# The last cross-attention of a two-layer decoder: exponentials and values split into leads and rests, products with the values in three single passes

## The reference

```python
x = _layernorm(x, ln_media_w, ln_media_b)          # the 77 context rows
lat = _layernorm(latents, ln_lat_w, ln_lat_b)      # the 512 decoder positions
q = lat @ Wq + bq
kv_in = jnp.concatenate([x, lat], axis=1)          # 589 keys and values
kv = kv_in @ Wkv + bkv
k, v = jnp.split(kv, 2, axis=-1)
...
sim = jnp.einsum('bhid,bhjd->bhij', q * scale, k)  # 16 heads of width 64
sim = sim - jax.lax.stop_gradient(jnp.max(sim, axis=-1, keepdims=True))
attn = jax.nn.softmax(sim, axis=-1)
out = jnp.einsum('bhij,bhjd->bhid', attn, v)
...
return out @ Wout + bout
```

## Time and profile before

| | |
|---|---|
| three runs | 1129.16, 1139.89, 1142.47 us; median 1139.89 |
| the profiled execution | 1145.58 us, span 1143.9 us |
| first step to last step of the pipeline | about 418 to 1056 us of the span |
| PE busy over the span | 1060.7 us, 93% |
| DVE, ACT, POOL busy | 724.1, 577.2 and 248.6 us |
| chain of work that ended last, share by engine | PE 85%, DVE 10%, ACT 3%, POOL 1% |

### The profile page before, as it was taken

How to read it: one execution, slowest core, us unless ns; L and a number is a source line. 1 busy time by engine, 2 the same in 40 slices (tenths; PEclk the granted TensorE clock), 3 DMA queues, 4 the chain that set the end, 5 groups by cost and what they waited for, 6 DMA issues and landing times.

```text
span 1143.9 us, 14143 instructions
## 1 busy us (share of the span) xinstructions
PE 1060.7 (93%) x4746; PEld 734.1 (64%) x4746; DVE 724.1 (63%) x1640; ACT 577.2 (50%) x1057; POOL 248.6 (22%) x307
## 2 busy tenths in 40 slices
PE   6869999999999479999989999999999999999896
PEld 3648779888888256565657666676666676665532
DVE  5866575656656567768675776756767657752256
ACT  4336444342334345565554665646665646655453
POOL 6111220008447241212131111111111111110001
PEclk9978667999999679999999999999999999999998
DMA  7100000000001000000000000000000000000001
GB/s 230 7 1 1 1 1 1 1 1 1 1 1 37 1 1 1 1 1 0 1 1 1 1 1 1 1 1 1 1 1 1 1 1 1 1 1 1 1 0 38
DMA packets 15667, 9.87 MB, mean 9 GB/s; under 512 B 8760, under 2 KB 14828, under 8 KB 15084
## 3 DMA queue, kind: packets, MB, share of 16 engines
q1 hardware_dynamic: 15595, 8.96, 2.7%
HBM read 7.60 MB, written 1.05 MB: 8 GB/s over the span
## 4 chain that ended last, share of the span: by engine, by line
PE 85%; DVE 10%; ACT 3%; issue 1%; POOL 1%; POOLq 0%; DVEq 0%; ACTq 0%
PE PS L1459 81%; PE PS L1471 4%; DVE mxm L1349 1%; DVE st L988 1%; DVE X_ODD L999 1%; DVE X_EVEN L999 1%; DVE BIG L1082 1%; DVE mx L1079 1%; DVE QA L1292 1%; POOL rs L564 0%; DVE mv L991 0%; ACT BIG L725 0%; ACT BIG L717 0%; PE PS L1821 0%; DVE VXA L1308 0%
## 5 line engine op out<-in xcount | busy, mean ns | idle before, releaser
L1459 PE MATMUL PS<-BIG,VXA 128*128 128x512 f32 (+1 forms) x640 | 335.6, 606 | 0.0
L943 ACT ACTIVATE BIG<-PS 128x512 f32<-128x512 f32 (+1 forms) x320 | 189.7, 593 | 136.0 <-PE PS L1459 126.0
L1349 DVE TENSOR_REDUCE mxm<-PS 128x1 f32<-128x512 f32 x256 | 170.6, 687 | 95.7 <-PE PS L1459 91.1
L1459 PE MATMUL PS<-QA,KA 128*128 128x512 f32 (+1 forms) x320 | 194.8, 609 | 0.0
L1459 PEld LDWEIGHTS PS<-BIG,VXA 128*128 128x128 f32 (+1 forms) x640 | 115.2, 190 | 29.4 <-ACT BIG L943 8.5
L1459 PE MATMUL PS<-QB,KB 128*128 128x512 f32 (+1 forms) x320 | 126.2, 394 | 0.0
L1459 PE MATMUL PS<-KA,QA 128*128 128x512 f32 (+1 forms) x512 | 118.0, 333 | 8.0 <-DVE mxm L1349 7.0
L905 ACT ACTIVATE KA<-PS,b1s 64x78 fp32r<-64x78 f32 (+1 forms) x128 | 64.3, 502 | 90.9 <-PE PS L1459 89.2
L1459 PEld LDWEIGHTS PS<-KA,QA 128*128 128x128 f32 x512 | 86.5, 190 | 31.8 <-DVE mxm L1349 11.7
L666 POOL CAST KA<-KA 64x78 fp32r<-64x78 f32 (+1 forms) x128 | 55.0, 429 | 205.2 <-ACT KA L905 201.4
L666 POOL CAST QB<-QA 64x512 fp32r<-64x512 f32 x64 | 39.0, 609 | 268.8 <-ACT QA L905 268.6
(11 more groups left out here) (251 smaller groups left out, 1791.5 us busy)
## 6 DMA issues: line engine op xcount, KB each, us to landing
X_EVEN<-in_x SPq DMA_DIRECT2D x4, 256.0 KB, 3.3
VXA<-in_L_ffn_Wg SPq DMA_DIRECT2D x1, 1024.0 KB, 5.7
VXA<-in_L_ffn_Wu SPq DMA_DIRECT2D x1, 1024.0 KB, 7.7
VXA<-in_L_ffn_Wd SPq DMA_DIRECT2D x1, 1024.0 KB, 9.3
REG<-in_L_xattn_Wkv SPq DMA_DIRECT2D x1, 1024.0 KB, 4.7
QB<-crow SPq DMA_DIRECT2D x64, 2.0 KB
out<-X_EVEN SPq DMA_DIRECT2D x4, 256.0 KB, 2.3
wq1s<-in_L_xattn_Wq SPq DMA_DIRECT2D x1, 512.0 KB, 8.5
```

The lines of the kernel that those rows point to most:

```text
L943: act.activation(PX[0:rows, g % 4, :], PS[0:rows, g % 2, :], ACT.Exp, scale=SCALE_W).then_inc(pw_ready, 1)
L1349: dve.tensor_reduce(mxm[:, p % 2, h, m:m + 1], PS[:, 2 + g % 2, :], AX.X, ALU.max).then_inc(mu_free, 1)
L1459: return pe.matmul(dst, lhsT, rhs, start=start, stop=stop, **kw)
```

## The change

- **Exponentials.** Each slot's exponential is still written as float32 (`PX`), and now also as a lead `PHI` of type `fp32r`. In six of the ten slots ACT makes it by a second `Exp` of the same scores (`lead_act`); in slots 2, 3, 7 and 8 (`LEAD_ON_VECTOR`) DVE makes it by a copy of `PX`. POOL subtracts the two into the rest `PLO` (`rest`), once per slot, behind that slot's `twins`.
- **Products with the values.** `pv` is three single-pass matmuls (value rest times `PHI`, value lead times `PHI`, value lead times `PLO`), and it comes three slots behind the scores (`LAG`). The third waits for POOL's `rest`. `s_wide` waits for ACT's second exponential of two slots before, where ACT makes one.
- **Values.** They are made a quarter of the heads at a time (256 columns), 20 tasks per sequence where there were 10 of 512 columns. ACT writes their lead (`value_lead`), DVE the rest (`value`).
- **Places.** `c` moves from slot 6 to 7, `yE` from 6 to 8, the inverse sums (`HEAD_SLOTS`) from slots 2 and 7 to 3 and 8, and the maximum units are spread so that two of them come before their step.

```diff
-HEAD_SLOTS = {2: 1, 7: 0}
-MAX_UNITS = {0: [0], 1: [1, 2], 2: [3, 4], 3: [5, 6], 4: [7], 5: [8, 9]}
+LAG = 3
+HEAD_SLOTS = {3: 1, 8: 0}
+MAX_UNITS = {0: [2], 1: [3], 2: [4], 3: [5], 4: [6], 5: [7, 8], 6: [9], 8: [0], 9: [1]}
+LEAD_ON_VECTOR = (2, 3, 7, 8)
...
-        t[6] = [("c", p + 1)]
+        t[7] = [("c", p + 1)]
...
+    ahead = p // 2 + 1
+    if ahead < B * QUARTERS:
+        for j, slot in ((0, 2), (1, 7), (2, 8)) if p % 2 == 0 else ((3, 2), (4, 7)):
+            t.setdefault(slot, []).append(("V", ahead, j))
...
+            def rest(g):
+
+                p, slot = divmod(g, SLOTS)
+                rows = min(P, KEYS - P * (slot % KB))
+                pool.wait_ge(pw_ready, g + 1)
+                if slot in LEAD_ON_VECTOR:
+                    pool.wait_ge(lead_dve, leads(g)[1])
+                else:
+                    pool.wait_ge(lead_act, leads(g)[0])
+                pool.tensor_tensor(PLO[0:rows, g % 4, :], PX[0:rows, g % 4, :], PHI[0:rows, g % 4, :].bitcast(F32), ALU.subtract).then_inc(rest_ready, 1)
+                pool.wait_ge(rest_ready, g + 1)
...
                         if key[0] in ("Q", "K", "Kt"):
                             twins(key)
+                    rest(SLOTS * p + slot)
...
                     act.activation(PX[0:rows, g % 4, :], PS[0:rows, g % 2, :], ACT.Exp, scale=SCALE_W).then_inc(pw_ready, 1)
+                    if slot not in LEAD_ON_VECTOR:
+                        act.activation(PHI[0:rows, g % 4, :], PS[0:rows, g % 2, :], ACT.Exp, scale=SCALE_W).then_inc(lead_act, 1)
                     for key, h in splits(tasks, slot):
                         hi(key, h)
+                    for key in tasks.get(slot, []):
+                        if key[0] == "V":
+                            value_lead(key)
...
+            def lead(g):
+
+                rows = min(P, KEYS - P * (g % KB))
+                dve.wait_ge(pw_ready, g + 1)
+                dve.tensor_copy(PHI[0:rows, g % 4, :], PX[0:rows, g % 4, :]).then_inc(lead_dve, 1)
...
-                    pe.wait_ge(pw_ready, g - 1)
+                    if (slot - 2) % SLOTS in LEAD_ON_VECTOR:
+                        pe.wait_ge(pw_ready, g - 1)
+                    else:
+                        pe.wait_ge(lead_act, leads(g - 2)[0])
...
-                mm(PS[:, 4 + h, :], value_and_ones(j, hp, h, rows), PX[0:rows, g % 4, :], start=j == 0, stop=j == KB - 1).then_inc(pv_ready, 1)
+                v_hi, v_lo = (with_sums(values, j, p, h, rows) for values in (VHI, VLO))
+                p_hi, p_lo = PHI[0:rows, g % 4, :], PLO[0:rows, g % 4, :]
+                mm(PS[:, 4 + h, :], v_lo, p_hi, start=j == 0, stop=False)
+                mm(PS[:, 4 + h, :], v_hi, p_hi, start=False, stop=False)
+                pe.wait_ge(rest_ready, g + 1)
+                mm(PS[:, 4 + h, :], v_hi, p_lo, start=False, stop=j == KB - 1).then_inc(pv_ready, 1)
```

More of the change, by code:

```diff
@@ L32 @@
 NHP = NH // 2
-HALF = NHP // 2
+QUARTERS = NHP // 2
 PAIRS = B * NHP
@@ L183, with max_units, leads @@
 STEPS = PAIRS
-HEAD_SLOTS = {2: 1, 7: 0}
-MAX_UNITS = {0: [0], 1: [1, 2], 2: [3, 4], 3: [5, 6], 4: [7], 5: [8, 9]}
+LAG = 3
+HEAD_SLOTS = {3: 1, 8: 0}
+MAX_UNITS = {0: [2], 1: [3], 2: [4], 3: [5], 4: [6], 5: [7, 8], 6: [9], 8: [0], 9: [1]}
+LEAD_ON_VECTOR = (2, 3, 7, 8)
+def max_units(p, slot):
+    first = p + 2 if slot > 7 else p + 1
+    return [(first, u) for u in MAX_UNITS.get(slot, []) if first < PAIRS]
+def leads(g):
+    p, slot = divmod(g, SLOTS)
+    on_vector = len(LEAD_ON_VECTOR) * p + sum(s <= slot for s in LEAD_ON_VECTOR)
+    return g + 1 - on_vector, on_vector
 OD_STEPS = {(0, 8): (1, 0), (0, 9): (1, 1), (2, 9): (2, 0), (3, 9): (2, 1), (5, 9): (3, 0), (6, 9): (3, 1)}
@@ L200, in step_tasks @@
     if p + 1 < PAIRS:
-        t[6] = [("c", p + 1)]
+        t[7] = [("c", p + 1)]
     b, hp = divmod(p, NHP)
[L203 to L207, removed]
+    ahead = p // 2 + 1
+    if ahead < B * QUARTERS:
+        for j, slot in ((0, 2), (1, 7), (2, 8)) if p % 2 == 0 else ((3, 2), (4, 7)):
+            t.setdefault(slot, []).append(("V", ahead, j))
     if b and hp == 0:
-        t[6].append(("yE", b - 1))
+        t[8].append(("yE", b - 1))
     for slot in range(8, SLOTS):
@@ L361, in decoder @@
         LATHI, LATLO = over("LATHI", x_odd_at, [P, B, S]), over("LATLO", xt_at, [P, B, S])
+        VHI, VLO = (over(name, vxa_at + 4 * 2 * KB * 2 * 3 * DW * n, [P, 2, KB, 2, 3, DW]) for n, name in enumerate(("VHI", "VLO")))
+        PHI, PLO = over("PHI", vxa_at + 4 * 2 * 2 * KB * 2 * 3 * DW, [P, 4, S]), over("PLO", big_at, [P, 4, S])
         DG = Y[:].rearrange("p b t d -> p b (t d)")
@@ L905, in hi, with value_lead @@
                 act.activation(dst, PS[own, 6 + n % 2, 0:width], ACT.Identity, bias=bias).then_inc(hi_ready, 1)
+            def value_lead(key):
+                _, ahead, j = key
+                n = PJ[key]
+                rows = min(P, KEYS - P * j)
+                if ahead == 0 and j == 0:
+                    act.wait_ge(setup_done, N_E_OPERANDS)
+                if ahead >= 2 and j == 0:
+                    act.wait_ge(pv_ready, SLOTS * 2 * (ahead - 1))
+                act.wait_ge(pj_full, n + 1)
+                act.activation(VHI[0:rows, ahead % 2, j, :, 0:3:2, :],
+                               PS[0:rows, 6 + n % 2, 0:4 * DW].rearrange("p (c n d) -> p c n d", c=2, n=2), ACT.Copy).then_inc(vhi_ready, 1)
             def lat_lead(b):
@@ L1398, in _ @@
                             task(key)
+                    if slot in LEAD_ON_VECTOR:
+                        lead(SLOTS * p + slot)
             head_out(2 * PAIRS - 1)
```

78 lines of the change are left out of this document (38 added, 40 removed).

## The result

The changed kernel takes 1190.52 us (median of four runs, 1177.6 to 1193.35), the kernel before 1141.18 us (four runs) on the same chip. The ratio is 1.0447, with a 95% interval of 1.0323 to 1.0571. The profiled executions compare 1190.13 us with a span of 1188.4 to 1145.58 with a span of 1143.9, a difference of 44.5 us in the span. The ratios are of undisturbed runs; a few single runs took far longer (5435.47 us once in four of the kernel without rests, 1198.27 and 1955.97 us in ten of the one with the power functions first) and are not in them.

What follows compares the result with a forecast made beforehand. The prediction took PE's own passes to bound the kernel before, at 18.68 us a step. Its terms summed to +45.5 us on the profiled 1145.6, carried as 1139.9 + 45 = 1185 us, 4% slower, range 1112 to 1225.

Steps and rivals of the forecast that it cites:

- K chain: From the `K` task's end through ACT and POOL to slot 6's third `pv` pass: 6.25 us, PE standing 1.6.
- Q chain: ACT and POOL work for `Q` delaying slot 0's rest, needed in slot 3: PE waits 1.3 or 0.6 us, mean 0.95.
- ordinary steps without `yE`: Pipeline steps without special work: 19.85 us each instead of 18.68, +28 us over 24 steps.
- three with `yE`: Three steps with `yE` inside give ACT and POOL 7 us to catch up: -4 us.
- steps 1, 4, 7: Normalising steps: power functions wait behind POOL's rests, eight normalisations meet POOL's lock; +4 us each, +12 together.
- steps 9, 17, 25: Pipeline steps with one normalisation: +2.7 us each, +8 together.
- drain behind the last transpose: End of the pipeline: three slots drained instead of one, with a subtraction among them; +1.5 us.
- PE's own sum: PE's passes over the ten slots of a step: 17.1 us if nothing makes PE wait.
- ACT at 17 us: Sign in the profile after: ACT should be at 17 us of a step; its load was summed to 17.3.
- PE keeps the bound: Rival: leads come in time and PE saves 51 us, giving 1090 us; chance 0.08 in full, 0.10 in part.
- POOL's throughput decides: Rival: POOL's load sets steps of 18.0 to 18.7 us, chains half overlap, giving 1148 us; chance 0.22.
- DVE becomes the bound: Rival: each DVE copy waits the full 1.27 us for POOL, steps about 21 us, giving 1226 us; chance 0.10.

Runs made afterwards that it cites:

- the kernel without rests: Changed kernel with POOL's rests of the exponentials left out and PE's third `pv` pass using `PHI` again: 1124.48 us, ratio 0.9803.
- the one with the power functions first: Changed kernel with inverse sums one slot later, plus POOL's normalisation power functions ahead of that slot's rest: 1147.22 us, ratio 1.0056.
- The sums moved by one slot: Changed kernel with `HEAD_SLOTS` 3 to 4: ACT's odd-head inverse sums, and DVE's scaling behind them, one slot later: 1148.22 us, ratio 1.0.
- the lag of two: Changed kernel with `LAG` 2 instead of 3, value products two slots behind the scores: 1397.59 us, ratio 1.2225.
- copy first: Later inverse sums and one-input `cmx`, plus DVE's `PHI` copy ahead of normalisations and tasks: 1176.32 us; with the `c` row before the copy, 1161.93 us.
- copy first only there: Later inverse sums and one-input `cmx`, plus DVE's `PHI` copy early only in steps that normalise, `c` row before it: 1161.97 us, ratio 1.0212.

## Why the prediction was right, and where its sizes were off

**The mechanism.** The forecast was that PE would stand at the third pass because the order of ACT's and POOL's lists makes the rest late. The sums moved by one slot (-42 us) and the rests left out (-66) each took the stall of the K chain away, and the lag of two made it larger. The -42 us are not the K chain's alone, since the same edit also ended the wait for the maxima. The K chain was forecast at 6.25 us and took 6.12. Its one mis-sized link is ACT's pair of exponentials: 0.62 was taken for each, and their starts are 0.50 apart (874.32 and 874.82). PE's pass time ahead of the third pass was 5.3 and not 4.64 us, in part because PE first waited 0.43 for a maximum (876.45 is 0.66 behind the pass before it). So the stall at this place was 0.8 and not 1.6 us; part of the missing time had gone into the wait before it. The Q chain's wait was there too (a third pass at 890.74, 0.6 behind the one of 890.14, so 0.37 late).

Over eight ordinary steps the third pass comes late by these amounts, in us a step:

| slot | forecast | measured |
|---|---|---|
| 6 (K chain) | 1.6 | 0.80 |
| 3 (Q chain) | 0.95 (0.6 and 1.3 by turns) | 0.31 (0.22 to 0.41) |
| 7 | 0.2 | 0.11 |

All three slots were named rightly and in the right order, and each was priced at about twice the measured wait or more.

**The terms, on the two profiled executions** (steps from transpose to transpose):

| term | forecast | measured |
|---|---|---|
| ordinary steps without `yE` | +24.5 (21 of the forecast's 24) | +20.5 |
| three with `yE` | -0.5 (3.5 as ordinary steps, less 4) | +1.0 |
| steps 1, 4, 7 | +12 | +8.8 |
| steps 9, 17, 25 | +8 | +8.6 |
| last step | 0 | -1.1 |
| drain behind the last transpose | +1.5 | +2.0 |
| prologue, from `LATLO` to the first transpose | 0 | +1.7 |
| unchanged code ahead of `LATLO` | 0 | +3.1 |
| sum | +45.5 | +44.5 |

The sum is better than its parts, and that is luck. Ordinary steps and steps 1, 4 and 7 were over-forecast, and what they lacked was made up by the steps with `yE` and by two terms that I had at 0: the prologue, and the code before the pipeline, in which nothing changed and which took 3.1 us more in this execution. What lengthened the prologue is open; with `soft` behind the values it was no shorter. The steps with `yE` did let ACT and POOL catch up, but by 0.7 us each and not by 1.3: they were +0.3 us each where the other ordinary steps were +1.0, and -1.1 in the kernel with the sums one slot later, so stalls were left in them too. In the special steps a cost came in that the forecast had left out, the clock: two of the intervals behind a `yE` are 21.71 and 21.72 us, and the third, in which passes ran 0.43 us apart from 673.7 to 675.9, is 22.63.

**PE's own sum was too low.** 17.1 us a step was forecast if nothing waits. Without any rest the step is 17.8, of which some 0.4 is the wait for DVE's maxima; with the later sums it is 18.04, of which 0.4 is late third passes. So PE's own share is 17.4 to 17.6. This error of +0.3 to +0.5, with the wait for the maxima that the forecast did not have, offsets most of the stalls that it had too large: 19.85 for 19.47 is closer than the parts are. The 0.16 us a slot for three passes in place of a float32 one stands (the third is 0.23 behind the second, the next scores 0.23 behind the third), but of the 1.6 us a step only 0.8 (18.61 to 17.8) is left. That narrow pieces and value tasks take back the part that isn't the wait for the maxima is what remains, and was not measured by itself.

**ACT's and POOL's loads.** Over six ordinary steps (841.10 to 957.77) ACT is drawn busy for 15.4 us a step and POOL for 16.2, where 17.3 and 18.0 were forecast. So the sign "ACT at 17 us" failed: ACT had slack, in part since its pairs of exponentials start closer together. POOL is near its 16.4 without waits: in ordinary steps it does not stand for DVE's copies, for which the forecast had added 0.4 each.

**The rivals.** *PE keeps the bound* was excluded by the waits of the result. *POOL's throughput decides* is what the sums one slot later might have been, as it takes the same time as before; but its steps are 18.04 with PE drawn at 97.5%, near the 17.8 of PE alone, so it isn't throughput that holds the ordinary steps. *DVE becomes the bound*: the copies do wait (0.72 in the mean for 0.41 alone), less than the 1 us that I took, but the copies aren't on the chain that held PE: they take as long in the kernel with the later sums (0.73), where the loss is gone. The Trainium skill (SBUF — State Buffer, "SBUF: two separate sides") has the lock for a DVE instruction in a two-port mode, or for one with two SBUF inputs against a GpSimd instruction that reads SBUF. The traces agree: the copy and the two-input maximum take up to 1.49 and 1.27 us beside POOL, the one-input reduction never more than 0.165. In which mode the copy runs, no run here shows.

**Why even the cured order wins nothing.** Kernel before against the one with the sums one slot later, from first to last transpose: 619.33 and 616.7 us. The first nine intervals cost +4.7, the three later steps with one normalisation +3.5, prologue and drain about +3 more; the three with `yE` give -3.4, the twelve steady ones -6.8, the last four -0.7. The gain of the passes is small, and the special steps hand it back. In them DVE's normalisations, POOL's power function and POOL's ten subtractions wait in one order for each other; three attempts at that order (power function first, copy first, copy first only there) made it no better, and in the last the lower clock behind PE's stands added to the loss. Whether another order does is open; I found no complete version that beats the kernel before.

## What to carry to other kernels

When work is added to engines that had room, price the longest chain from a producer through each queue to its deadline, with every instruction that stands ahead in the lists, before adding up busy times: here one slot's place of two functions on ACT, and of the scaling on DVE that hangs on them, was worth 42 us of 1190, with no instruction less. Look up every list that a constant moves work in, before calling an edit a test of one chain. Put on a shared queue first what has a deadline, but check what the early result sets free: a subtraction that starts sooner may run beside work that its port shuts out. A wait that goes away is often replaced by the next in line, so look at the view of waits again after every single move.

## What the runs showed of the hardware

- DVE's `cmx`, 4 elements a partition with two SBUF inputs, takes 0.84 us in the mean in the changed kernel, beside POOL's subtractions of 1.3, and 0.164 before the change; without the subtractions, but beside POOL's casts, it took 0.30. The form with one input takes 0.160 to 0.165 in all its 64 places. The duration of a tiny instruction can be its neighbour's.
- Two exponentials of ACT behind each other from the same PSUM bank start 0.50 us apart although each is drawn at 0.58 to 0.60.
- In the lag of two, the four windows from 600 to 1000 us have granted clocks of 0.81 to 0.87, with PE drawn 81 to 82% busy; in the changed kernel the one from 900 to 1000 us has 1.00, with 94%. Behind a single stand of 3.74 us (step 9, copy early) PE's passes started 0.43 us apart in place of 0.23 for some 7 us.
- The unchanged code ahead of the pipeline is not constant. `LATLO` starts at 398.78 before and 401.84 after, but at 383.08 and 396.22 in two experiments whose code there is alike, profiled in the same group of runs. Their windows of 110 to 200 us differ in the granted clock (0.87 and 0.75), with PE about as busy. The earlier one:

```profile
110.00:200.00 90.00, 84.52 (x567) 71.96 (x566) 66.07 (x204) 45.23 (x79) 19.01 (x17) 0.87 0.00 1
```

and the later one:

```profile
110.00:200.00 90.00, 85.94 (x528) 73.88 (x528) 58.85 (x173) 42.52 (x75) 19.02 (x17) 0.75 0.00 1
```

This is 13 us, more than most of the edits here are worth, and is why the steps of the pipeline were compared, and not the totals alone. The difference of 13 us is measured; that the clock made it is my reading of the two windows.
